# A gather of 127 rows with the 128th fetched by another queue, in a graph layer with 106,250 edges

## The reference

```python
seg = edge_dst * R + edge_type
S   = segment_sum(x[edge_src], seg, N * R).reshape(N, R, D)
cnt = segment_sum(1, seg, N * R).reshape(N, R)
agg = einsum('nrd,rdf->nf', S, relation_weights) + cnt @ rFeatures
h   = agg * deg(dst) ** -0.5
out = layernorm(x + relu(h + h @ loop_weight))
```

## Time and profile before

| | |
|---|---|
| three timed runs | 1353.03, 1357.11, 1358.55 us; median 1357.11 |
| profiled execution, its own time | 1360.85 us |
| its span, first to last instruction | 1359.0 us |
| mean granted clock of TensorE | 0.908 |
| busy: PE, POOL, VectorE, ACT | 1064.8, 821.6, 714.7, 523.5 us |
| DMA | 66256 packets, 127.17 MB, 94 GB/s in the mean |

### The profile page before, as it was taken

How to read it: one execution, slowest core, us unless ns; L and a number is a source line. 1 busy time by engine, 2 the same in 40 slices (tenths; PEclk the granted TensorE clock), 3 DMA queues, 4 the chain that set the end, 5 groups by cost and what they waited for, 6 DMA issues and landing times. The chain is left out here.

```text
span 1359.0 us, 25380 instructions
## 1 busy us (share of the span) xinstructions
PE 1064.8 (78%) x6713; PEld 932.1 (69%) x6713; DVE 714.7 (53%) x2570; ACT 523.5 (39%) x1119; POOL 821.6 (60%) x846
## 2 busy tenths in 40 slices
PE   2268887877887887788878887888887888778888
PEld 1157776766766776677777776777777777667777
DVE  6275554545455555555455554555455555545554
ACT  3054443433343433344333433343344333334333
POOL 7706666666666666666566656666566666656650
PEclk9989988989899899989879988998889899988989
DMA  9512333333323333333233323333333333333320
GB/s 287 149 66 86 91 89 88 89 94 88 90 86 96 85 92 93 89 86 94 82 93 90 90 84 91 90 90 91 88 86 93 91 90 92 91 92 86 90 87 16
DMA packets 66256, 127.17 MB, mean 94 GB/s; under 512 B 15828, under 2 KB 38446, under 8 KB 66110
## 3 DMA queue, kind: packets, MB, share of 16 engines
q0 software_dynamic: 39056, 105.51, 27.1%
q1 hardware_dynamic: 13022, 13.65, 3.2%
q10 hardware_dynamic: 14032, 6.35, 1.6%
HBM read 115.85 MB, written 9.60 MB: 92 GB/s over the span
## 5 line engine op out<-in xcount | busy, mean ns | idle before, releaser
L520 POOL DMA_INDIRECT rows<-x_parts,src x780 | 767.9, 984 | 478.1 <-issue 200.3
L615 ACT COPY ring<-win_ps 128x451 f32 x831 | 466.7, 562 | 758.8 <-remote 455.2
L1067 PEld LDWEIGHTS agg_ps<-ring,w 128*128 128x128 f32 x3936 | 614.8, 208 | 187.5 <-issue 137.6
L1067 PE MATMUL agg_ps<-ring,w 128*128 128x128 f32 x3936 | 641.9, 293 | 118.2 <-issue 116.8
L1055 PE MATMUL win_ps<-hot,rows 128*128 128x480 f32 x1662 | 621.0, 458 | 37.9 <-issue 37.1
L949 DVE TENSOR_TENSOR ring<-ring,win_ps 128x41 f32 x831 | 186.1, 224 | 623.5 <-ACT ring L615 515.0
L817 DVE TENSOR_SCALAR hot<-iota,key_f 128x480 fp32r<-128x480 f16 x831 | 391.0, 471 | 0.7 <-issue 0.7
L1055 PEld LDWEIGHTS win_ps<-hot,rows 128*128 128x128 f32 x1662 | 283.0, 211 | 57.7 <-issue 54.0
L1047 PEld LDWEIGHTS win_ps<-hot_node,hot_type 128*128 128x128 bf16 x831 | 76.9, 104 | 151.2 <-issue 95.4
L1047 PE MATMUL win_ps<-hot_node,hot_type 128*128 128x12 bf16 x831 | 88.6, 173 | 114.2 <-DVE ring L949 51.3
L527 POOL DMA_INDIRECT raw<-x,src x51 | 51.8, 1016 | 22.2 <-issue 15.0
(11 more groups left out here) (89 smaller groups left out, 227.6 us busy)
## 6 DMA issues: line engine op xcount, KB each, us to landing
rows<-x_parts,src POOLq DMA_INDIRECT x780
x_parts<-x_out SPq DMA_DIRECT2D x6, 512.0 KB
x_parts<-ring SPq DMA_DIRECT2D x6, 512.0 KB
out<-out_sb ACTq DMA_DIRECT2D x48, 64.0 KB
x_blk<-x ACTq DMA_DIRECT2D x47, 64.0 KB
w<-relation_w SPq DMA_DIRECT2D x8, 320.0 KB
x_in<-x SPq DMA_DIRECT2D x6, 256.0 KB
ring<-x SPq DMA_DIRECT2D x6, 256.0 KB
```

What stands on the lines that cost most here:

```text
L520: pool.indirect_dma_start(rows[0:n, k].rearrange("p c d -> p (c d)").bitcast(F32), None, x_parts, bass.IndirectOffsetOnAxis(ap=src[0:n, t: ...
L615: nc.scalar.copy(ring[:, :, bass.ds(start + 1, WIN - 1)], win_ps[bank_of(t)][:, :, 1:WIN]).then_inc(copied, 1)
L1067: ins = nc.tensor.matmul(sums_of(c), w[:, r, :], ring[:, r, bass.ds(seg, BLOCK)], start=(r == 0), stop=(r == COLS - 1))
```

## The change

From tile 51 on POOL gathers only the first 127 rows of a full tile. Row 128 comes from SP: the host passes the source index of each tile's last edge as an extra input, `src_ends`. SP loads these 830 numbers into `end_src`; VectorE multiplies them by 1024 (bytes of a row) into `end_at`. SP reads up to 32 of them at a time into registers and issues one transfer of 1 KB for each tile, after the same wait for `tile_done` as POOL's. PE waits for `end_landed[k]` after `gathered[k]`. `BEHIND` goes from 5 to 11, so that the addition of tile t waits for gather t + 11 from t = 24 on. The last tile, of ten rows, is gathered as before.

```diff
-BEHIND = 5
+BEHIND = 11
+BY_POOL = P - 1
+ROW_LOAD = 32
+ROW_BYTES = 2 * D * 4
...
+        x_bytes = x_parts.bitcast(U8).rearrange("n b -> (n b)").unsqueeze(0)
...
+            sp.wait_ge(ends_cleared, 1)
+            sp.dma_start(end_src[0:whole, :], ...).then_inc(ends_loaded, 16)
+            sp.dma_start(end_src[whole:whole + 1, 0:more], ...).then_inc(ends_loaded, 16)
...
+                for b in range(STAGE_BUFS):
+                    sp.wait_ge(staged[b], stage_count(b) * 16)
+                sp.wait_ge(ends_ready, 1)
+                end_rows()
+
+            def end_rows():
+                for first in range(PLAIN // ROW_LOAD * ROW_LOAD, FULL, ROW_LOAD):
+                    ts = range(max(first, PLAIN), min(first + ROW_LOAD, FULL))
+                    index = [sp.alloc_register(f"sp_end{t}") for t in ts]
+                    sp.load(index, end_at[first // ROW_LOAD:first // ROW_LOAD + 1, ts[0] - first:ts[-1] + 1 - first])
+                    for t, reg in zip(ts, index):
+                        k = t % TPB
+                        sp.wait_ge(tile_done, t - TPB + 1)
+                        at_least(sp, end_landed[k], (t - PLAIN) // TPB * 16)
+                        at = sp.snap(reg, donate=True)
+                        sp.dma_start(rows[BY_POOL:P, k].rearrange("p c d -> p (c d)").bitcast(U8),
+                                     x_bytes[:, bass.ds(at, ROW_BYTES)]).then_inc(end_landed[k], 16)
...
-                n = rows_in_tile(t)
+                n = min(rows_in_tile(t), BY_POOL)
...
+            nc.vector.memset(end_src[:], 0).then_inc(ends_cleared, 1)
...
+                dve.wait_ge(ends_loaded, 2 * 16)
+                nc.vector.tensor_scalar(end_at[:], end_src[:], float(ROW_BYTES), None, ALU.mult).then_inc(ends_ready, 1)
...
                     pe.wait_ge(gathered[k], gathers_into(k, t) * 16)
+                    if t < FULL:
+                        pe.wait_ge(end_landed[k], ((t - PLAIN) // TPB + 1) * 16)
```

More of the change, by code:

```diff
@@ L117, in bank_of, with build @@
     return BANK_OF["tile", t]
-def build(nc, x, src_main, src_rest, dst_main, dst_rest, type_main, type_rest, r_features, relation_w, loop_w, out):
+def build(nc, x, src_main, src_rest, dst_main, dst_rest, type_main, type_rest, src_ends, r_features, relation_w, loop_w, out):
     with ExitStack() as ctx:
@@ L168, in build @@
         iota_i = piece(R * WIN).bitcast(I32)
+        end_src = sb("end_src", [-(-FULL // ROW_LOAD), ROW_LOAD], I32)
+        end_at = sb("end_at", [-(-FULL // ROW_LOAD), ROW_LOAD], I32)
+        x_bytes = x_parts.bitcast(U8).rearrange("n b -> (n b)").unsqueeze(0)
         zeros = sb("zeros", [P, COLS, WIN], F32)
@@ L268, in build @@
         gather_issued = sem("gather_issued")
+        ends_cleared = sem("ends_cleared")
+        ends_loaded = sem("ends_loaded")
+        ends_ready = sem("ends_ready")
+        end_landed = [sem(f"end_landed{k}") for k in range(TPB)]
         gathered = [sem(f"gathered{k}") for k in range(TPB)]
@@ L456, in _ @@
                 stage_load(n)
+            sp.wait_ge(ends_cleared, 1)
+            whole, more = divmod(FULL, ROW_LOAD)
+            sp.dma_start(end_src[0:whole, :], src_ends[:, 0:whole * ROW_LOAD].rearrange("o (m n) -> (o m) n", n=ROW_LOAD)).then_inc(
+                ends_loaded, 16)
+            sp.dma_start(end_src[whole:whole + 1, 0:more], src_ends[:, whole * ROW_LOAD:FULL]).then_inc(ends_loaded, 16)
             sp.dma_start(loop[:], loop_w).then_inc(loop_loaded, 16)
@@ L480, in in_order @@
                         w_load((n - 3) * W_LOAD)
+                for b in range(STAGE_BUFS):
[14 more added lines that the diff above has]
+                                     x_bytes[:, bass.ds(at, ROW_BYTES)]).then_inc(end_landed[k], 16)
+                    for reg in index:
+                        sp.free_register(reg)
             def g_load(t):
@@ L1202 @@
         arrays[f"{name}_rest"] = np.ascontiguousarray(a[FULL * P:].reshape(REST, 1))
+    arrays["src_ends"] = np.ascontiguousarray(np.asarray(src)[:FULL * P].reshape(FULL, P)[:, P - 1].reshape(1, FULL))
     arrays["r_features"] = np.ascontiguousarray(L0_gnn_rFeatures)
```

## The result

The changed kernel takes **2353.53 us** (median of 4 runs, 2351.88 to 2355.6), where the kernel before, run beside it, takes 1357.83. The ratio is 1.7295, with a 95% interval of 1.7247 to 1.7342. The forecast of 1200 us is wrong, and so is its range of 1130 to 1390.

The account below looks back on a forecast made before the run. PE was taken as the bound, with idle holes and a low clock; halving both gives 100.7 + 779 x 1.342 + 37.5 = 1184, plus 13 for PE's added wait 1197 of span, 1195 against the median, said as 1200; range 1130 to 1390.

Parts of the forecast that it names:

- 127 rows instead of 128: POOL's gather: row count worth next to nothing, 0.5 ns a row; 127 rows likely dealt to one engine, three in four.
- Rival C: POOL's gather or its one engine too slow: over 1.27 us is slower than today, at 1.5 us 1540; chance 0.13.
- successive gathers are not put on the same one: DMA engines: gathers take the engines in turn; on the same engine it would be 780 x 7.3 us = 5700 us.
- the threshold of 11: VectorE's addition waiting for gather t + 11: 0 with 15 ahead; binds without cost in rate once POOL sets the pace.
- A landing of 5 to 7 us: Sign of being right: a gather's rows land 5 to 7 us after its start.
- fewer shares: Sign of being right in queue 0: fewer, fuller shares, over 32 data packets' worth on one engine.
- Half the holes go: PE's idle "issue" gaps at L1067: half go, with half the low clock, giving 1.117 + 0.225 = 1.342 us a tile.
- PE's own pace: PE's time per tile without holes and low clock: 1.567 - 0.293 - 0.157 = 1.117 us.
- PE's second wait, 13 us: One more wait instruction per tile in PE's sequencer, 51 ns each: 13 us, bounds 0 and 40.
- SP's transfers: SP's 779 transfers of 1 KB: 0.32 us issue each, SP keeps up, nothing added to the sum.

Follow-up runs that it names:

- part 3: Threshold of 11 and SP's transfers into an unread buffer, 128 rows by POOL, against the kernel before on a quick chip: ratio 1.0045.

## Why the prediction was wrong

**The step that failed** is the first sentence of "127 rows instead of 128": "For POOL the number of rows is worth next to nothing", with 0.5 ns a row. The duration of the gather was carried over as 0.984 us; measured are 2.542. The two rows it rests on, 0.886 us for ten rows and 0.949 for 128, are right, but they were divided by the wrong thing. Ten rows are one row on each of ten engines, 128 are eight on each of sixteen: the 63 ns are seven rows of *share*, 9 ns each, and not 118 rows (that ten rows are dealt to ten engines is read from the 32 packets, 16 x (1 + 1), and the divisor). The prediction itself put the share of 127 rows at 127, three in four likely, and a line later asked only what one engine's *transfer* would take. With its own numbers, 0.949 + 119 x 0.009 = 2.02 us, POOL's pace would have been 2.32 us a tile and the span 100.7 + 779 x 2.32 + 37.5 = 1945 us: 17% short, on the right side.

**Rival C** named the mechanism ("POOL's gather with one ring of 127"), its threshold of 1.27 us and the right formula; with 2.542 instead of 1.5 us it gives 100.7 + 779 x 2.842 + 37.5 = 2352 against a span of 2350.3. Its size of 1.5 us had no row behind it, and what spoke against it ("ten rows and 128 rows cost POOL nearly the same") was the same misreading. The range ended at 1390, below C's own 1540.

**Right:** 127 rows go through one engine; successive gathers are not put on the same one (at 7.3 us each it would have been 5700 us); the threshold of 11 cost nothing while 15 gathers were ahead, and once POOL sets the pace it binds and costs nothing in rate. The six tiles behind the last gather (part 3) are what this leaves out. **Wrong beside it:** A landing of 5 to 7 us was too short, it takes 10.3 (median, on a quick chip). And queue 0 did not show fewer shares, since the engines without a row get as many packets.

**Half the holes go.** They all went, for another reason than the one given. If a gather held up instructions on the engine that it shares with them, gathers on all 16 engines every 1.65 us should leave some holes; with 300 columns there are none. Nor is there one hole for each packet of queue 8, which the prediction took for PE's instructions: from 300 to 1300 us the trace of the kernel before has 41 such packets and 66 groups of gaps (gaps over 0.25 us, less than 4 us apart), 1 to 25 us behind the last packet. What PE is short of on such a chip is a rate, one tile in 1.55 to 1.59 us, and POOL now asks for less. What limits the rate stays open; that it is the supply of instructions fits the stalls of several engines in the opening and was not shown.

**PE's own pace** of 1.117 us a tile stands within 3%: on a chip without holes PE is busy for 640.88 / 560 = 1.144 us a tile.

**PE's second wait, 13 us.** Nothing, as its lower bound had it, where it was run alone. The sum of all the rest is 17 us, within the bounds of 0 to 40, but on a quick chip SP's transfers together with the threshold took 5 us that were put at 0, by the traces the threshold's six tiles.

## What to carry to other kernels

For a gather that POOL issues, work out the share of the busiest engine before touching the number of rows: rows divided by their largest divisor up to 16. POOL's cost rises with that share, and all sixteen engines get the packets for it, so 127 rows cost POOL 2.7 times what 128 do (2.542 against 0.949 us). When two rows of a trace are divided to give a price per unit, ask which quantity really differs between them.

And one execution is one chip: idle time named "issue", for nothing that the profile shows, may be the chip's and not the kernel's; have the kernel before run beside each experiment.

## What the runs showed of the hardware

- The same kernel takes 1076.5 us on two chips and 1345 to 1363 us on the others, with a clock of 0.99 and 0.91. On the slower ones several engines stand still on "issue" in the opening, and PE's rate ends at 628 to 645 tiles in 1000 us. Where POOL asks for 629 or fewer there are neither holes nor a low clock down to 603 tiles (0.98 to 0.99). With 509 tiles (122 rows) it is 0.92, and with 352 tiles, where PE is busy for 62% of the time, 0.70.
- A gather of 127 rows has 528 packets instead of 48, and 480 of them are under 512 B and carry no row.
- A gather takes POOL 952 ns (median) with a clear of 150 columns behind it, but 1192 ns with one of 220 (both on both kinds of chip) and 1124 ns with one of 300. No run says why; it is also why 220 columns cost 219 us more than 150 on a quick chip, where the clear itself is only 58 ns longer.
- A wait that is already met costs PE nothing on a quick chip: 779 of them, ratio 0.9992 (0.9983 to 1.0002).
- An addition that waits for gather t + 11 instead of t + 5 keeps VectorE six tiles further behind POOL where POOL sets the pace (540 additions instead of 546 up to 700 us), and 6.2 us longer are needed behind the last gather.
